# A routed pair of adapter layers: VectorE's step in another order, the raw down weight fetched two steps ahead, and the order of items counted from item 0's adapter

## What is computed

```python
def layer(role, x, Wd, bd, Wu, bu, gamma, beta):      # R = 3 adapters, H = 1024, K = 512, fp32
    h = gelu(einsum('bsh,bhk->bsk', x, Wd[role]) + bd[role][:, None, :])
    y = x + einsum('bsk,bkh->bsh', h, Wu[role]) + bu[role][:, None, :]
    yn = (y - mean(y)) * rsqrt(var(y) + 1e-5)
    return yn * gamma[role][:, None, :] + beta[role][:, None, :]
x = layer(itok, x, L0...); x = layer(itok, x, L1...)
```

## Time and profile before

| | us |
|---|---|
| median of 3 runs (2803.05 to 2805.55) | 2804.37 |
| the profiled execution | 2803.86 |
| its span, first to last instruction | 2802.0 |
| TensorE busy | 2700.2 |
| VectorE, ScalarE, GpSimd busy | 2194.5, 1702.5, 1344.6 |
| mean granted clock of TensorE, share of full | 0.987 |

### The profile page before, as it was taken

The page is one execution under the profiler, slowest core; times in us unless marked ns, Lnnn a source line. Parts: engine busy times, 40 slices in busy tenths (PEclk is TensorE's granted clock), DMA queues, the critical chain, the costliest instruction groups (busy, mean ns, idle before and its releaser), DMA issues.

```text
span 2802.0 us, 57328 instructions
## 1 busy us (share of the span) xinstructions
PE 2700.2 (96%) x11714; PEld 2208.4 (79%) x11714; DVE 2194.5 (78%) x3341; ACT 1702.5 (61%) x2907; POOL 1344.6 (48%) x1050
## 2 busy tenths in 40 slices
PE   6999999999999999999989999999889999999997
PEld 5788888877788888888778787878667887878785
DVE  4777776768777776777898888888888888888886
ACT  4566665666666665656656566656555566666564
POOL 0455555544555555555444444444434444444446
PEclk9999999999999999999999999999999999999998
DMA  6665666666665666666776665666676665666664
GB/s 189 199 209 199 212 209 207 212 218 219 204 223 199 212 209 207 208 204 211 217 223 202 192 222 190 214 198 201 198 210 204 211 204 189 214 201 204 197 202 145
DMA packets 365915, 573.60 MB, mean 205 GB/s; under 512 B 40960, under 2 KB 240768, under 8 KB 365440
## 3 DMA queue, kind: packets, MB, share of 16 engines
q1 hardware_dynamic: 365440, 569.61, 62.9%
HBM read 364.97 MB, written 204.47 MB: 203 GB/s over the span
## 4 chain that ended last, share of the span: by engine, by line
PE 73%; issue 9%; DVE 9%; DVEq 2%; ACT 2%; DMA 2%; SPq 1%; POOL 1%; ACTq 0%; POOLq 0%
PE pD L463 38%; PE bX L475 20%; PE bZ L475 15%; DVE xt L842 2%; DVEq L221 2%; DMA cbd<-in_bd 1%; DVE hl L824 1%; DVE xt L865 1%; DVE wul L743 1%; ACT pC L625 1%; DVE xl L802 1%; DVE xt L834 1%; DVE xT L795 1%; ACT xh L573 1%; SPq L269 0%
## 5 line engine op out<-in xcount | busy, mean ns | idle before, releaser
L415 POOL TENSOR_TENSOR xt<-xt,cgb 128x1024 f32<-128x1024 f32 x260 | 649.7, 2500 | 419.5 <-ACT xt L633 419.5
L463 PE MATMUL pD<-wdh,xh 128*128 128x512 f32 x2080 | 814.3, 392 | 11.1 <-ACT pD L588 10.4
L463 PE MATMUL pD<-wdl,xh 128*128 128x512 f32 x2080 | 813.2, 391 | 0.0
L463 PE MATMUL pD<-wdh,xl 128*128 128x512 f32 x2080 | 812.6, 391 | 0.0
L633 ACT ACTIVATE xt<-xt,rstd 128x1024 f32<-128x1024 f32 x260 | 298.8, 1150 | 459.2 <-POOL rstd L408 380.8
L463 PEld LDWEIGHTS pD<-wdh,xh 128*128 128x128 f32 x2080 | 393.3, 189 | 95.2 <-issue 11.2
L865 DVE SCALAR_TENSOR_TENSOR xt<-xt,nmean,cgb 128x1024 f32<-128x1024 f32 x260 | 462.3, 1778 | 0.8 <-POOLq L435 0.8
L463 PEld LDWEIGHTS pD<-wdl,xh 128*128 128x128 f32 x2080 | 393.3, 189 | 82.0
L463 PEld LDWEIGHTS pD<-wdh,xl 128*128 128x128 f32 x2080 | 392.8, 189 | 82.4
L475 PE MATMUL bX<-wuh,hh 128*128 128x512 f32 x1040 | 412.2, 396 | 45.7 <-DVE xt L834 22.4
L625 ACT ACTIVATE pC<-xt,nmean 128x512 f32<-128x512 f32 x520 | 359.8, 692 | 137.8 <-DVE nmean L850 73.4
(11 more groups left out here) (90 smaller groups left out, 3746.1 us busy)
## 6 DMA issues: line engine op xcount, KB each, us to landing
xq<-in_xB SPq DMA_DIRECT2D x130, 512.0 KB, 3.6
htok<-hg SPq DMA_DIRECT2D x260, 256.0 KB, 2.8
hq<-htok SPq DMA_DIRECT2D x1040, 64.0 KB, 2.2
xt<-in_x SPq DMA_DIRECT2D x130, 512.0 KB, 4.2
mid<-xt SPq DMA_DIRECT2D x130, 512.0 KB, 3.6
xq<-mid SPq DMA_DIRECT2D x520, 128.0 KB, 3.2
xt<-mid SPq DMA_DIRECT2D x130, 512.0 KB, 4.3
out<-xt SPq DMA_DIRECT2D x130, 512.0 KB, 2.7
```

The source lines that it names most:

```text
L415: eng.tensor_tensor(xt[:, k, :], xt[:, k, :], cgb[:, 1, :], ALU.add).then_inc(s_o, 1)
L463: last = eng.matmul(pD[e][:, :], a[:, e, 128 * k:128 * k + 128], w[:, k, :], start=False, stop=(k == 7 and n == 2), skip_group_check=True)
```

## The change

Five things: SP fetches the first pair's bias and down weight as soon as the first item's adapter `c_first` is known, and the first x block at once; adapters are counted modulo 3 from item 0's adapter in the sort (`rq`); at a new phase the raw down weight is fetched one step earlier (`when_new(eng, i + 2, down_weights)` at the end of step i), the bias where it was; VectorE's order within `begin` and `end` is another, with `t4` moved from `take_wu_1` to `factors`; and the first pair's up weight is taken whole at the end of `end(1)` on ScalarE and VectorE (`when_next` is `when_new` without the first pair). Besides, TensorE clears `pD` ahead of the ordering's matmuls, and ScalarE calls Gelu once on one column ahead of everything.

```diff
@@ SP
             def down_weights(p):
-                row, c = adapter(p), pd.next()
+                down_row(adapter(p))
+
+            def down_row(row):
+                c = pd.next()
                 eng.wait_ge(f_rd, c + 1)
                 for h in range(2):
                     for a in range(4):
...
+
+            def down_bias(p):
+                row = adapter(p)
                 count(eng, s_sd, p + -1, 2, 2)
                 eng.dma_start(cbd[:, :], bd[row, :].broadcast_to([128, K])).then_inc(s_bd, 16)
...
-            load_blocks(Pair(0), 0)
-            down_weights(Pair(0))
+
+            eng.wait_ge(s_first, 1)
+            row = bass.ds(eng.value_load(c_first[0:1, 0:1], min_val=0, max_val=2), 1)
+            eng.dma_start(cbd[:, :], bd[row, :].broadcast_to([128, K])).then_inc(s_bd, 16)
+            down_row(row)
+            eng.wait_ge(s_ctl, 1)
...
                 if not (i + 1).first():
-                    when_new(eng, i + 1, down_weights)
+                    when_new(eng, i + 1, down_bias)
...
                 if not v.first():
                     when_new(eng, v, up_biases)
+                when_new(eng, i + 2, down_weights)
@@ ScalarE: end
-                when_new(eng, w, take_wu_1)
+                when_next(eng, w, take_wu_1)
                 square(u, 0, 0)
                 square(u, 0, 1)
                 high_h(w, 3)
                 square(u, 1, 0)
                 square(u, 1, 1)
+                if i.j is None and i.c == 1:
+                    take_wu_0(Pair(0))
+                    take_wu_1(Pair(0))
+                    take_wu_2(Pair(0))
@@ VectorE: ordering
             link(eng.tensor_scalar(rf[:, :], tf[:, :], 0.0, 2.0, ALU.max, ALU.min))
-            eng.tensor_scalar(z0[:, :], rf[:, 0:NB], 0.0, None, ALU.is_equal).then_inc(s_p, 1)
-            eng.tensor_scalar(z1[:, :], rf[:, 0:NB], 1.0, None, ALU.is_equal).then_inc(s_p, 1)
-            eng.scalar_tensor_tensor(out=kf[:, 0:NB], in0=rf[:, 0:NB], scalar=float(NB), in1=io[:, 0:NB],
+            eng.tensor_copy(c_first[:, :], rf[0:1, 0:1]).then_inc(s_first, 1)
+
+            link(eng.tensor_scalar(rq[:, :], rf[:, :], rf[:, 0:1], None, ALU.subtract))
+            link(eng.tensor_scalar(tf[:, :], rq[:, :], 0.0, 3.0, ALU.is_lt, ALU.mult))
+            link(eng.tensor_tensor(rq[:, :], rq[:, :], tf[:, :], ALU.add))
+            eng.tensor_scalar(z0[:, :], rq[:, 0:NB], 0.0, None, ALU.is_equal).then_inc(s_p, 1)
+            eng.tensor_scalar(z1[:, :], rq[:, 0:NB], 1.0, None, ALU.is_equal).then_inc(s_p, 1)
+            eng.scalar_tensor_tensor(out=kf[:, 0:NB], in0=rq[:, 0:NB], scalar=float(NB), in1=io[:, 0:NB],
...
@@ VectorE: factors, take_wu_1
                 eng.tensor_tensor(t2, b22, b12, ALU.subtract).then_inc(s_sub, 1)
                 eng.wait_ge(s_sub, c * 4 + 2)
-                eng.sem_inc(s_seen, 1)
+                eng.tensor_tensor(t4, b21, t2, ALU.subtract).then_inc(s_sub, 1)
...
                 c = pg[1].next()
                 low_wu(c * 7, 2, t2)
                 low_wu(c * 7, 3, b22)
-                eng.tensor_tensor(t4, b21, t2, ALU.subtract).then_inc(s_sub, 1)
                 eng.wait_ge(s_wul, c * 7 + 1)
                 eng.tensor_tensor(b11, t2, b11, ALU.subtract).then_inc(s_sub, 1)
                 eng.wait_ge(s_wul, c * 7 + 4)
@@ VectorE: begin, end
                 u, w = i + -3, i + -2
                 transpose_h(w, 0)
                 transpose_h(w, 1)
-                onto(u, 1, bX[u.c % 2], 0, 0)
                 when_new(eng, i, take_wd_1)
                 ready(i, s_wd[1])
+                onto(u, 1, bX[u.c % 2], 0, 0)
                 low_x(i, 1)
                 onto(u, 2, bZ, 1, 1)
                 low_h(w, 0)
-                when_new(eng, u, take_wu_2)
+                when_next(eng, u, take_wu_2)
                 ready(u, s_wu[2])
-                when_new(eng, w, factors)
+                when_next(eng, w, factors)
 
             def end(i):
                 u, w = i + -3, i + -2
@@ -885,26 +919,31 @@
                 onto(u, 3, X, 0, 1)
                 variance(u + -1)
                 scale(u + -1, 0)
+                scale(u + -1, 1)
+                low_h(w, 1)
+                last_onto(u, 4, bZ, 0, 1, 3)
                 transpose_x(i + 1, 0)
-                low_h(w, 1)
-                when_new(eng, w, take_wu_0)
+                when_next(eng, w, take_wu_0)
                 ready(w, s_wu[0])
                 ready(w, s_cb)
-                last_onto(u, 4, bZ, 0, 1, 3)
-                scale(u + -1, 1)
                 last_onto(u, 5, X, 1, 1, 2)
                 low_x(i + 1, 0)
                 last_onto(u, 6, bZ, 0, 0, 1)
                 mean(u, 0, 6)
+                transpose_x(i + 1, 1)
                 when_new(eng, i + 1, take_wd_0)
                 ready(i + 1, s_wd[0])
-                transpose_x(i + 1, 1)
                 low_h(w, 2)
-                when_new(eng, w, take_wu_1)
-                ready(w, s_wu[1])
                 last_onto(u, 7, X, 1, 0, None)
                 mean(u, 1, 7)
                 low_h(w, 3)
+                when_next(eng, w, take_wu_1)
+                ready(w, s_wu[1])
+                if i.j is None and i.c == 1:
+                    factors(Pair(0))
+                    take_wu_0(Pair(0))
+                    take_wu_1(Pair(0))
+                    take_wu_2(Pair(0))
 
             steps(eng, halves(begin, end), -1, NPH + 5, 0)
```

More of the change, by code:

```diff
@@ L229, in when_new, with when_next @@
                     do(p)
+        def when_next(eng, p, do):
+            if not p.first():
+                when_new(eng, p, do)
         class Phases:
@@ L443, in _ @@
         def _(eng):
+            eng.wait_ge(s_zero, 1)
+            for bank in pD:
+                last = eng.matmul(bank[:, :], zero[:, 0:128], zero[:, 0:K], start=True, stop=True)
+            last.then_inc(s_bits, 1)
             eng.wait_ge(s_oh, 2)
@@ L447, in _ @@
                        skip_group_check=True).then_inc(s_pc, 1)
-            eng.wait_ge(s_zero, 1)
-            for bank in pD + bX:
-                eng.matmul(bank[:, :], zero[:, 0:128], zero[:, 0:K], start=True, stop=True)
-            eng.matmul(bZ[:, :], zero[:, 0:128], zero[:, 0:K], start=True, stop=True).then_inc(s_bits, 1)
+            for bank in bX + [bZ]:
+                last = eng.matmul(bank[:, :], zero[:, 0:128], zero[:, 0:K], start=True, stop=True)
+            last.then_inc(s_bits, 1)
             def down(i, e, q):
@@ L513, in _ @@
         def _(eng):
+            eng.wait_ge(s_id, 2)
+            eng.activation(gelu_set[:, :], mhalf[:, :], ACT.Gelu)
             eng.wait_ge(s_ctl, 1)
@@ L586, in seed_d @@
                 if p.exists():
+                    if p.first():
+                        eng.wait_ge(s_bits, 1)
                     count(eng, s_hg, p + -1, 2, e + 1)
@@ L591, in seed_x @@
                 if p.exists():
+                    if p.first():
+                        eng.wait_ge(s_bits, 2)
                     count(eng, s_cb, p, 1, 1)
```

21 lines of the change are left out of this document (11 added, 10 removed).

## The result

The changed kernel takes **2840.41 us** (median of 4 runs, 2838.63 to 2844.38) against 2804.96 of the kernel before beside it (2803.05 to 2805.58): a ratio of 1.0128, interval 1.0116 to 1.0140. It is 1.3% slower. The forecast was 2804, no change, with a range of 2790 to 2817. The profiled execution has a span of 2836.9 us, 34.9 more than that of before.

What follows compares the result with a forecast made beforehand. TensorE, busy 96% with 73% of the chain, was taken as the bound, so its standstills count. Terms -12.8 + 5.6 - 3.6 + 0 + 8.5 + 2 = -0.3 us against 2803.9 gave 2804 us, no change; range 2790 to 2817.

Steps and rivals of the forecast that it cites:

- part 4: Down weight at the three later phases: earlier fetch ends ScalarE's waits, `onto` 1 comes late; sum 0, bounds -9 and +6.
- Part 1: Layer 1's nine turns: `scale` 1 escapes POOL, PE's wait for `last_onto` 5 goes; -12.8 us, bounds -8 and -17.
- Part 2: Layer 0's eight turns: the added `scale` delays `last_onto` 4, 0.7 us each; +5.6 us, bounds +2 and +6.5.
- Part 3: Start: PE starts 9.3 us earlier, then waits 12.3 us behind the up weight's block; -3.6 us, bounds -9 and +1.
- Part 5: Up weight at the three later phases: VectorE's new order meets POOL's additions and idles; +8.5 us, bounds +1 and +14.
- Part 6: The rest: order of items, extra ordering operations, Gelu's table load and one more SP branch per step; 0 us.
- the tail: Kernel's end: the added `scale` ahead of `last_onto` 4 lands on PE, three steps at 0.7; +2 us, bounds 0 and +3.5.
- B: Rival, slower: VectorE's new order collides with POOL in the up weight's steps, at `take_wu_0` and `cbu`; 2815.5 us, chance 0.26.

Runs made afterwards that it cites:

- e1: The changed kernel with already-met waits put on VectorE ahead of layer 1's loop, its head 8 instructions further on; 2812.12 us, ratio 1.0028.
- e8: The kernel before with VectorE's new order in the second half of a step for layer 1's pairs alone; 2791.75 us, ratio 0.9953.
- e2: The kernel before with met waits over VectorE's steps 60 to 69, putting layer 1's loop head 5 instructions ahead of a block's end; 2838.16 us, ratio 1.0110.
- e6: e5 with product 0's addition first, the first pair's up weight taken part by part, and loop turns moved off the 2 MB fetch; 2797.31 us, ratio 0.9971.
- e10: The changed kernel keeping the early first fetch, VectorE's new order only in layer 1 up to the last pair, head moved, bias ahead of the down weight; 2779.43 us.
- e11: e10 with VectorE's loops of twelve pairs instead of six, so that it turns about half as often; 2780.18 us, ratio 0.9915.
- e12: e6 with the down bias issued ahead of x's block and h's second reading on SP; 2788.92 us, ratio 0.9947.
- e3: The changed kernel with the raw down weight fetched at its old place, one step ahead, the bias behind it; 2836.20 us, ratio 1.0110.
- e4: The changed kernel with product 0's addition (`onto` 1) ahead of the down weight's second half again; 2833.31 us, ratio 1.0105.
- e5: e1 with VectorE's second half of a step in the old order for layer 0, the new order kept for layer 1; 2803.47 us, ratio 0.9996.
- e7: The kernel before with only the raw down weight fetched two steps ahead, the bias where it was; 2814.20 us, ratio 1.0035.

## Why the prediction was wrong

Of the 34.9 us of span, 26.6 are the place of the loop's head (34.9 less e1's 8.3), which no term of the sum held. Without it the kernel would have come out at e1's 2812: inside the range, but still slower than before (1.0015 to 1.0041), 8 us above the forecast, and that is mostly part 4.

**Part 1, turns of layer 1 (-12.8): the mechanism right, the result turned round.** The step that failed is "Up to `last_onto` 4 VectorE loses `transpose_x` 0 (1.25) and gains a `scale` (1.28), so PE's wait for that result stays". It did not stay: it was 0.6 us at each of the nine turns and became 2.4 to 2.7. The durations were right (1.278 on average for the 260). What the step counted was work, and what it left out was that the same instructions, moved in the code, ran dry 5 instructions into the turn: 1.76 to 2.01 us, nine times, and a low clock behind seven of them. With the head elsewhere, e1's seven quiet turns give -12.9, e8's -13.1, a little more than forecast. The Trainium skill, Runtime: NRT & Kernel Launch, section "Instruction fetch mechanics", has the first half of this: a taken branch whose target lies outside the two pages that an engine holds must wait until that page is fetched. The trace agrees (3.46 us at 1599.00). The same section puts such a page at 16 KiB and calls the crossing of its boundary mostly hidden. Here the packets of queue q14 are of 8192 bytes (only the twelve of queue q8 have 16384), e2's end lies 128 instructions from the changed kernel's by the count in the built program, and the crossing costs 1.6 to 3.6 us when it comes just behind a jump.

**Part 2, turns of layer 0 (+5.6): right.** Six quiet turns lose 4.7 more, 0.8 each; 0.7 was forecast.

**Part 3, start (-3.6): right, -3.8.** PE starts at 20.03 (18.1 forecast), stops at 46.9 (44.6) and goes on at 56.94 (56.9), behind the up weight taken in one piece. PE's row there:

```profile
56.94 0.79 PE L483 MATMUL pD<-wdh,xh 128*128 128x512 f32 x1 [10.07 <-DVEq L820]
```

The kernels that take it part by part have -5.6 to -7.5 for the stage (e6, e10, e11, e12), those that take it whole -1.5 to -4.3 (the changed kernel, e1, e3, e4, e5): the block gave back about half of what the early fetch won.

**Part 4, down weight (0): wrong, about +12** (9.1 at pair 30 and 5.5 at pair 95, less 0.8 and 1.8 for the turns in these stages). One step was right: `onto` 1 behind `take_wd_1` comes 5.22 us late for PE (5.5 forecast), and e4 gets part of that back in each phase. Two failed. "The bias ... no longer queues behind them": it does, by way of h, whose write lands behind the 2 MB while SP waits for it (5.1 us in e6; with the bias ahead of that wait, in e12, ScalarE's waits of 6.05 and 8.91 us for it are 0.38 and 1.07). And "they have over ten microseconds before their users, so nothing": this counted the users of data, and left out the engines' own code, which comes over the same DMA engines; a turn behind the 2 MB takes 7.3 to 8.3 us (taken out in e3, put in in e7).

**Part 5, up weight (+8.5): right in layer 0, wrong in layer 1.** Pair 30: +6.1, of it 0.8 a turn; 4.5 was forecast and e5 shows that the order is the cause. Pair 95: -1.9, and -3.3 with the head moved, where +2 was forecast. The working had named the reason, the luck at the port: two additions met at pair 30, one at pair 95, where `cbu` began 0.3 us ahead of POOL's second addition and took its quiet 0.68. Tenths of a microsecond decide which it is. The Trainium skill, SBUF — State Buffer, section "SBUF: two separate sides", says that whichever of the two engines' instructions starts first has the shared port pair to its end. The traces agree at both pairs (4.56 and 2.82 us at pair 30, 0.68 at pair 95); the prediction's step from that rule to both additions being met came true at one.

**Part 6 and the tail (0 and +2):** the tail is +4.3, beyond its bound of 3.5, and e10 takes it back with the old order behind the last pair. The order of items was not tried by itself. Two slips in the sum are too small to matter: 87.4 less 91.11 is -3.7, not -3.6, and the tail has 198 steps from matmul to matmul, not 199, so its loss before is 8.9, not 8.7.

**The rivals.** B had the right sign, and the collision that it rests on came at pair 30; but of 35 us it explains 6 (the up weight at pair 30). No rival had the code in it. The bounds of -8 and -17 on part 1 could not hold the result, because they bounded the size of work on VectorE, while the 4.80 us that VectorE idles at the turn were put down to the loop as something fixed.
